# A state-space recurrence inside a decoder kernel: two 512-column units of its elementwise products in one instruction, and two subtractions moved from VectorE to GpSimd

## The chip, the cores and the metric

The kernel runs on one core of one Trainium2 chip (trn2). The metric is the device time of one execution in microseconds (us); a run of the kernel is timed three times and the median counts. The engines are TensorE (PE: matrix products, into the eight banks of PSUM), VectorE (DVE), ScalarE (ACT), GpSimd (POOL) and SyncE (SP), on whose queue every DMA of this kernel is issued, in program order. Every engine works off its own program in order; a semaphore wait holds all that stands behind it on that engine.

## The reference, cut to what matters

The input has 4 x 512 positions of 512 features. The layer in question is a Mamba mixer; behind it come its MLP, a quantized product layer and an FFN with 4-bit weights, which the change does not touch.

```python
zxbcdt = x @ in_proj_w.T                      # z, xv, Bm, Cm, dt_in
dt = softplus(dt_in @ dt_proj_w.T + dt_proj_b)
dA = exp(dt[..., None] * A)
dtx = dt * x_full
dBx = dtx[..., None] * Bg                     # the drive
def step(h, inp):
    h = dA_i * h + dBx_i                      # 1024 channels x 16 states
    y = einsum(C_i, h)                        # the read-out
y = ys + D_skip * x_full
```

## The kernel before

**Phases.** Layer norm and the first projections (to about 78 us), then the recurrence with the projections of the later batches beside it (78 to 1062 us), then output projection, MLP, quantized layer and FFN. The change lies in the recurrence and the DMA order beside it.

**Units and steps.** The recurrence is cut into 512 units of 128 partitions x 512 positions: 32 steps `g` (4 batches x 8 channel tiles) of 16 units `c` each, `n = 16 g + c`. For a unit, `spread_v` (TensorE) spreads dt*x over the partitions into PSUM bank 2 or 3, `spread_dt` spreads dt into bank 0 or 1, `decay` (ScalarE, L847) turns that into exp(A dt) in place, `make_drive` (VectorE, L1349) multiplies bank 2 or 3 by B into the ring `drive`, `scan` (VectorE, L1358) runs the recurrence into the ring `state` (6 units), `read_out` (GpSimd, L1172) multiplies by C into the ring `read` (8 units), and `gather_four` (TensorE, L1784) sums four units over the states. Once a step `skip_y` (L1369) makes `y`, and `soft_rest` (L1338, tile `sp_rest`) is the last instruction of VectorE in a step.

**The chain to the next step.** During step `g` the operands of step `g + 1` are made: GpSimd does `soft_sum`, `soft_dt` (dt), `dt_x` (dt*x), `dt_low` and `v_low` (the low halves of both), ScalarE between its exponentials `dt_high` (L837) and `v_high` (L841). SyncE then copies the halves into `dpack` and `vpack` (eight DMAs: `load_pack_dt`, `load_pack_v`), and the first `spread_v` of the next step waits for all eight. Ahead of them in SyncE's order stands `weights_after(first + 1)`, which in steps 0 to 3 stores a freshly split weight tile (`store_w`, L469) and waits for its low half.

**Low halves.** TensorE takes float32 operands as a rounded high half (ScalarE, `w_high`, `split_hi`) and the difference (VectorE before the change: `w_low` L1324, 13 instructions in steps 0 to 4; `split_lo` L1319, 4 in each of steps 3, 11 and 19).

All orders are written out by hand in the loops; nothing is scheduled by a planner.

## Time and profile before

| | |
|---|---|
| median of three runs | 2874.28 us (2871.49 to 2877.53) |
| the profiled execution | 2876.27 us, its span 2874.5 us |
| recurrence within the span | 78 to 1062 us |
| VectorE busy in the recurrence | 956.94 of 984.00 us |
| GpSimd busy in the recurrence | 870.46 us |
| TensorE busy in the recurrence | 839.67 us, mean granted clock 0.87 |

A busy time is the time with an instruction of that engine under way; idle time counts only where other work waits for the engine.

### The profile page before, as it was taken

Reading aid. Unit: us, or ns where it says so; the run is one execution under the profiler, and the core shown is the slowest. Engines: PE = TensorE matmul, PEld = TensorE weight load, DVE = VectorE, ACT = ScalarE, POOL = GpSimd, SP = SyncE. Lnnn points to the kernel's source line nnn. Section 1 sums busy time; section 2 is a strip of 40 time slices with the busy share of each in tenths; the row PEclk is TensorE's granted clock in tenths of the full one; section 3 lists DMA queues with packets and bytes.
Section 4 is the critical chain, followed back from the end, with each engine's and each line's share of the span. In section 5 each row is a group of like instructions: output and inputs, shape, how many; then the busy total and the mean of one; then the engine's idle time right before and its main releaser. Section 6 shows DMA issues by size and latency. Waiting matters only on the chain.

```text
span 2874.5 us, 32445 instructions
## 1 busy us (share of the span) xinstructions
PE 2651.7 (92%) x11096; PEld 1880.8 (65%) x11096; DVE 2129.6 (74%) x2731; ACT 1152.1 (40%) x1690; POOL 1255.9 (44%) x836
## 2 busy tenths in 40 slices
PE   7888888888899878999999999999989999999999
PEld 3443444444344326788887777887877788888887
DVE  4999999999999985543366677777767865555563
ACT  4555555555555534432244443443333322222221
POOL 2789888888889871110010023222212522222220
PEclk8998998989889769999999999999999999999999
DMA  6654654554465436221111112112111111111111
GB/s 230 209 157 121 188 157 121 157 166 129 132 183 154 133 99 231 81 76 49 52 66 59 45 37 67 44 45 67 44 37 45 44 49 48 51 45 52 50 47 66
DMA packets 152310, 275.35 MB, mean 96 GB/s; under 512 B 27345, under 2 KB 27857, under 8 KB 151633
## 3 DMA queue, kind: packets, MB, share of 16 engines
q1 hardware_dynamic: 152144, 273.27, 31.5%
q8 instruction: 88, 1.44, 0.2%
q14 instruction: 78, 0.63, 0.1%
HBM read 178.01 MB, written 61.34 MB: 83 GB/s over the span
## 4 chain that ended last, share of the span: by engine, by line
PE 71%; DVE 11%; ACT 9%; issue 5%; POOL 2%; DMA 1%; SPq 1%; DVEq 0%; POOLq 0%; ACTq 0%
PE ps L1733 19%; PE ps L1734 18%; PE ps L1735 18%; PE ps L1772 8%; DVE state L1358 6%; ACT ps L847 5%; PE ps L1784 4%; POOL read L1172 1%; DMA uraw<-y_d 1%; PE ps L1924 1%; PE ps L1868 1%; PE ps L1898 1%; DVE drive L1349 1%; DVE act_o L1677 0%; POOL xhr L1217 0%
## 5 line engine op out<-in xcount | busy, mean ns | idle before, releaser
L1172 POOL TENSOR_TENSOR read<-state,c_t 128x512 f32<-128x512 f32 x512 | 664.0, 1308 | 138.2 <-DVE state L1358 118.5
L1358 DVE TENSOR_TENSOR_SCAN state<-ps,drive 128x512 f32<-128x512 f32 x512 | 622.3, 1216 | 14.3 <-ACT ps L847 12.8
L1733 PE MATMUL ps<-xh,ghi 128*128 128x512 f32 x1536 | 609.1, 397 | 5.7 <-issue 5.7
L1231 POOL TENSOR_TENSOR wdeq<-packed,scales 128x1024 f32<-128x1024 f16 x96 | 260.2, 2711 | 798.3 <-DVE packed L1510 798.3
L1735 PE MATMUL ps<-xh,glo 128*128 128x512 f32 x1536 | 599.3, 390 | 0.0
L1734 PE MATMUL ps<-xl,ghi 128*128 128x512 f32 x1536 | 599.2, 390 | 0.0
L847 ACT ACTIVATE ps<-ps,a_exp 128x512 f32<-128x512 f32 x512 | 338.9, 662 | 473.8 <-PE ps L1772 472.5
L1772 PE MATMUL ps<-dpack,sel 128*128 128x512 f32 x512 | 260.9, 510 | 114.2 <-DVE state L1358 112.1
L1677 DVE TENSOR_TENSOR act_o<-act_o,ps 128x512 f32<-128x512 f32 x192 | 131.7, 686 | 313.4 <-PE ps L1735 298.5
L1349 DVE TENSOR_TENSOR drive<-ps,b_t 128x512 f32<-128x512 f32 x512 | 344.1, 672 | 12.7 <-PE ps L1772 11.9
L1099 ACT ACTIVATE ahi<-act_o 128x512 fp32r<-128x512 f32 x192 | 121.4, 632 | 562.6 <-DVE act_o L1677 562.6
L1733 PEld LDWEIGHTS ps<-xh,ghi 128*128 128x128 f32 x1536 | 289.4, 188 | 68.7 <-issue 9.2
L1734 PEld LDWEIGHTS ps<-xl,ghi 128*128 128x128 f32 x1536 | 289.4, 188 | 62.1 <-issue 3.1
L1735 PEld LDWEIGHTS ps<-xh,glo 128*128 128x128 f32 x1536 | 289.1, 188 | 60.7
L1733 PE MATMUL ps<-ahi,ghi 128*128 128x512 f32 x768 | 306.3, 399 | 20.2 <-issue 20.2
L1735 PE MATMUL ps<-ahi,glo 128*128 128x512 f32 x768 | 300.6, 391 | 0.0
L1734 PE MATMUL ps<-alo,ghi 128*128 128x512 f32 x768 | 300.6, 391 | 0.0
L1772 PE MATMUL ps<-vpack,sel 128*128 128x512 f32 x512 | 251.3, 491 | 28.6 <-DVE drive L1349 16.7
L1663 DVE TENSOR_TENSOR res<-res,ps 128x512 f32<-128x512 f32 x192 | 130.9, 685 | 192.6 <-PE ps L1735 190.0
L1772 PEld LDWEIGHTS ps<-dpack,sel 128*128 128x128 f32 x512 | 107.8, 211 | 244.1 <-DVE state L1358 235.3
L1772 PEld LDWEIGHTS ps<-vpack,sel 128*128 128x128 f32 x512 | 105.8, 207 | 225.2 <-DVE drive L1349 115.3
L965 ACT ACTIVATE ghi<-wdeq 128x1024 fp32r<-128x1024 f32 x96 | 100.9, 1051 | 297.7 <-POOL wdeq L1231 266.0
(204 smaller groups left out, 3775.3 us busy)
## 6 DMA issues: line engine op xcount, KB each, us to landing
whi<-w_d SPq DMA_DIRECT2D x63, 256.0 KB, 4.1
wlo<-w_d SPq DMA_DIRECT2D x63, 256.0 KB, 4.6
dpack<-dh SPq DMA_DIRECT2D x64, 128.0 KB, 3.8
dpack<-dl SPq DMA_DIRECT2D x64, 128.0 KB, 3.6
b_d<-ev SPq DMA_DIRECT2D x32, 256.0 KB
x_d<-ev SPq DMA_DIRECT2D x32, 256.0 KB, 2.6
vpack<-vh SPq DMA_DIRECT2D x64, 128.0 KB, 3.5
vpack<-vl SPq DMA_DIRECT2D x64, 128.0 KB, 2.8
```

Of the source, the lines that this page charges most:

```text
L847: act.activation(ps[:, n % 2, :], ps[:, n % 2, :], ACT.Exp, scale=a_exp[:, col:col + 1]).then_inc(decay_ready, 1)
L1099: act.activation(ahi[n // 2][:, cols(n % 2)], act_o[n % 2][:, :], ACT.Copy)\
L1172: pool.tensor_tensor(read[:, n % RRING, :], state[:, n % SRING, :], c_t[:, g % 2, :], ALU.mult).then_inc(read_ready, 1)
L1231: pool.tensor_tensor(wdeq[:, :].rearrange("p (h n) -> p h n", h=2), codes, scale, ALU.mult).then_inc(deq, 1)
L1349: dve.tensor_tensor(drive[:, n % DRING, :], ps[:, 2 + n % 2, :], b_t[:, g % 2, :], ALU.mult).then_inc(drive_ready, 1)
L1358: dve.tensor_tensor_scan(state[:, n % SRING, :], ps[:, n % 2, :], drive[:, n % DRING, :], 0.0, ALU.mult, ALU.add)\
L1663: dve.tensor_tensor(res[:, f, cols(b)], res[:, f, cols(b)], ps[:, free_bank(24 * E + 16 + k), :], ALU.add).then_inc(added, 1)
L1677: dve.tensor_tensor(act_o[n % 2][:, :], act_o[n % 2][:, :], ps[:, free_bank(24 * E + 2 * n + 1), :], ALU.mult)\
L1733: pe.matmul(out_, w_h, x_h, start=(start and k == 0), stop=False)
L1734: pe.matmul(out_, w_h, x_l, start=False, stop=False)
L1735: last = pe.matmul(out_, w_l, x_h, start=False, stop=(stop and k == n - 1))
L1772: pe.matmul(ps[:, bank, :], sel[:, 4 * (j % 2) + m, :], pack[j // 2][:, :], start=True, stop=True).then_inc(done, 1)
```

## The change

`make_drive` and `read_out` work on two units (a pair, `m` or `k`, 1024 columns) in one instruction; their semaphores count pairs (`PAIRS`, 8 a step). `spread_v` is issued for both units of the next pair at even `c`. `w_low` and `split_lo` inside the recurrence are GpSimd's now. On GpSimd `soft_dt` follows `soft_sum` behind pair 0, `dt_x` stands behind pair 1, `dt_low` behind pair 2, `v_low` behind pair 3. On ScalarE `dt_high` stands behind the exponential of unit 4 (it was 5), `v_high` behind that of unit 6 (it was 7). `drive` holds twice as much, for which `v_t`, `vh`, `vl` and the softplus tiles share places, with waits that follow from it. Two sums on the input tiles (`normalise`) move from steps 2 and 4 to 5 and 7.

```diff
 STEPS = B * CT
...
+    drive = place("drive", [P, DRING, 2, S], F32, after())
     state = place("state", [P, SRING, S], F32, after())
...
-    vh = place("vh", [P, S], F32R, after())
+    assert after() <= NORM_END, (after(), NORM_END)
+    vh = place("vh", [P, S], F32R, SP + 8192)
     vl = place("vl", [P, S], F32R, after())
-    assert after() <= NORM_END, (after(), NORM_END)
+    assert after() <= SP_END
 
 
...
@@ -801,12 +805,14 @@
                 act.wait_ge(dtp_ready, q + 1)
                 if q:
                     act.wait_ge(sp_exp_ready, q)
+                    act.wait_ge(sp_sum_ready, q)
...
-                    act.wait_ge(dt_ready, q)
+                    act.wait_ge(v_ready, q)
+                    act.wait_ge(dl_ready, q)
...
             def soft_log(q):
                 if q:
-                    act.wait_ge(dt_ready, q)
+                    act.wait_ge(vl_ready, q)
...
@@ -915,9 +921,9 @@
                     if jobs and c % 4 == 2 and c > 4:
                         take(first + c // 4 - 1)
                     if 0 <= g + 1 < STEPS:
-                        if c == 5:
+                        if c == 4:
                             dt_high(g + 1)
-                        if c == 7:
+                        if c == 6:
                             v_high(g + 1)
                     if nb < B:
                         if c == 12:
@@ -1130,17 +1136,12 @@
             def soft_dt(q):
                 pool.wait_ge(sp_sum_ready, q + 1)
                 pool.wait_ge(sp_pos_ready, q + 1)
-                if q:
-                    pool.wait_ge(dl_ready, q)
-                    pool.wait_ge(v_ready, q)
                 pool.tensor_tensor(dt_t[:, :], sp_log[:, :], sp_pos[:, :], ALU.add)\
                     .then_inc(dt_ready, 1)
 
             def dt_x(q):
                 pool.wait_ge(dt_ready, q + 1)
                 pool.wait_ge(x_t_loaded[q % 3], x_loads(q))
-                if q:
-                    pool.wait_ge(vl_ready, q)
                 pool.tensor_tensor(v_t[:, :], dt_t[:, :], x_t[:, q % 3, :], ALU.mult)\
                     .then_inc(v_ready, 1)
...
@@ -1160,17 +1161,31 @@
                 pool.tensor_tensor(owlo[:, part, :], owraw[:, part, :], owhi[:, part, :].bitcast(F32),
                                    ALU.subtract).then_inc(owlo_ready, 1)
 
-            def read_out(g, c):
-                n = NST * g + c
+            def read_out(g, k):
+
+                n = NST * g + 2 * k
                 if n == 0:
                     pool.wait_ge(res_stored, 16)
-                if c == 0:
+                if k == 0:
                     pool.wait_ge(c_loaded[g % 2], 16 * (g // 2 + 1))
-                pool.wait_ge(scan_done, n + 1)
+                pool.wait_ge(scan_done, n + 2)
                 if n >= RRING:
                     pool.wait_ge(gathered, (n - RRING) // 4 + 1)
-                pool.tensor_tensor(read[:, n % RRING, :], state[:, n % SRING, :], c_t[:, g % 2, :],
-                                   ALU.mult).then_inc(read_ready, 1)
+                at, src = n % RRING, n % SRING
+                pool.tensor_tensor(read[:, at:at + 2, :], state[:, src:src + 2, :],
+                                   over_tiles(c_t[:, g % 2, :], 2), ALU.mult).then_inc(read_ready, 1)
+
+            def split_lo(b, f):
+                pool.wait_ge(ln_hi, FT * b + f + 1)
+                pool.tensor_tensor(xl[b][:, f, :], xlr[b][:, f, :], xh[b][:, f, :].bitcast(F32),
+                                   ALU.subtract).then_inc(ln_lo, 1)
+
+            def w_low(n):
+                pool.wait_ge(whi_ready, n + 1)
+                pool.wait_ge(wlo_ready, n)
+                pool.tensor_tensor(wlo[n % 3][:, :, :], wraw[:, n % 2, :, :],
+                                   whi[n % 3][:, :, :].bitcast(F32), ALU.subtract)\
+                    .then_inc(wlo_ready, 1)
 
...
@@ -1182,22 +1197,27 @@
             for f in range(FT):
                 normalise(1, f)
             for g in range(STEPS):
-                for c in range(NST):
-                    read_out(g, c)
-                    if g in (2, 4) and c % 4 == 3:
-                        normalise(1 + g // 2, c // 4)
-                    if g in (STEPS - 3, STEPS - 2) and c in (12, 14):
-                        out_weights_low(2 * (g - STEPS + 3) + (c - 12) // 2)
+                nb, k_, jobs = step_jobs(g)
+                first = IN_TILES * nb + 3 * k_
+                for k in range(PAIRS):
+                    read_out(g, k)
+                    if g in (5, 7) and k % 2 == 1:
+                        normalise((g - 1) // 2, k // 2)
+                    if g in (CT - 5, 2 * CT - 5, 3 * CT - 5) and k % 2 == 1:
+                        split_lo(g // CT + 1, k // 2)
+                    if g in (STEPS - 3, STEPS - 2) and k in (6, 7):
+                        out_weights_low(2 * (g - STEPS + 3) + k - 6)
+                    if jobs and k % 2 == 1 and k < 6 and first + k // 2 + 2 < IN_TILES:
+                        w_low(first + k // 2 + 2)
                     if g + 1 < STEPS:
-                        if c == 0:
+                        if k == 0:
                             soft_sum(g + 1)
-                        if c == 1:
                             soft_dt(g + 1)
-                        if c == 2:
+                        if k == 1:
                             dt_x(g + 1)
-                        if c == 6:
+                        if k == 2:
                             dt_low(g + 1)
-                        if c == 8:
+                        if k == 3:
                             v_low(g + 1)
...
-            def make_drive(g, c):
-                n = NST * g + c
-                if c == 0:
+            def make_drive(m):
+
+                g = m // PAIRS
+                if m % PAIRS == 0:
                     dve.wait_ge(b_loaded[g % 2], 16 * (g // 2 + 1))
-                dve.wait_ge(vb_ready, n + 1)
-                if n >= DRING:
-                    dve.wait_ge(scan_done, n - DRING + 1)
-                dve.tensor_tensor(drive[:, n % DRING, :], ps[:, 2 + n % 2, :], b_t[:, g % 2, :],
+                dve.wait_ge(vb_ready, 2 * m + 2)
+                if m >= DRING:
+                    dve.wait_ge(scan_done, 2 * (m - DRING + 1))
+                dve.tensor_tensor(drive[:, m % DRING, :, :], ps[:, 2:4, :], over_tiles(b_t[:, g % 2, :], 2),
                                   ALU.mult).then_inc(drive_ready, 1)
...
-            def scan(g, c):
-                n = NST * g + c
-                dve.wait_ge(drive_ready, n + 1)
+            def scan(n):
+                dve.wait_ge(drive_ready, n // 2 + 1)
                 dve.wait_ge(decay_ready, n + 1)
                 if n >= SRING:
-                    dve.wait_ge(read_ready, n - SRING + 1)
+                    dve.wait_ge(read_ready, (n - SRING) // 2 + 1)
                 dve.tensor_tensor_scan(state[:, n % SRING, :], ps[:, n % 2, :],
-                                       drive[:, n % DRING, :], 0.0, ALU.mult, ALU.add)\
+                                       drive[:, n // 2 % DRING, n % 2, :], 0.0, ALU.mult, ALU.add)\
                    .then_inc(scan_done, 1)
...
-            make_drive(0, 0)
+            make_drive(0)
             for g in range(STEPS):
                 nb, k, jobs = step_jobs(g)
-                first = IN_TILES * nb + 3 * k
                 for c in range(NST):
-                    if c + 1 < NST:
-                        make_drive(g, c + 1)
-                    elif g + 1 < STEPS:
-                        make_drive(g + 1, 0)
-                    scan(g, c)
+                    n = NST * g + c
+                    if c % 2 == 0 and n // 2 + 1 < PAIRS * STEPS:
+                        make_drive(n // 2 + 1)
+                    scan(n)
                     for b in (1, 2, 3):
                         if g == CT * b - 6 and c % 4 == 1:
                             scale_x(b, c // 4)
-                        if g == CT * b - 5 and c % 4 == 2:
-                            split_lo(b, c // 4)
                     if g >= 1 and c == 6:
                         skip_y(g - 1)
-                    if jobs and c % 4 == 3 and c < 12 and first + c // 4 + 2 < IN_TILES:
-                        w_low(first + c // 4 + 2)
                     if nb and jobs and k == 0 and c == 6:
                         dt_split(nb)
...
                 if n >= 2:
-                    pe.wait_ge(drive_ready, n - 1)
+                    pe.wait_ge(drive_ready, n // 2)
...
             spread_v(0)
+            spread_v(1)
             for g in range(STEPS):
                 nb, k, jobs = step_jobs(g)
                 first = IN_TILES * nb + 3 * k
                 for c in range(NST):
                     n = NST * g + c
-                    if n + 1 < NST * STEPS:
-                        spread_v(n + 1)
+                    if c % 2 == 0 and n + 2 < NST * STEPS:
+                        spread_v(n + 2)
+                        spread_v(n + 3)
                     spread_dt(n)
                     if jobs and c < 12:
                         project(first + c // 4, c % 4)
```

GpSimd in step 1, before: from the last read-outs of step 0 on (`read` is `read_out`, `sp_log`, `dt_t`, `v_t`, `dl`, `vl` are the results of `soft_sum`, `soft_dt`, `dt_x`, `dt_low`, `v_low`).

```order
L1127 TENSOR_TENSOR sp_log<-sp_log,sp_rest 128x512
L1172 TENSOR_TENSOR read<-state,c_t 128x512
L1136 TENSOR_TENSOR dt_t<-sp_log,sp_pos 128x512
L1172 TENSOR_TENSOR read<-state,c_t 128x512
L1144 TENSOR_TENSOR v_t<-dt_t,x_t 128x512
L1172 TENSOR_TENSOR read<-state,c_t 128x512 x4
L1149 TENSOR_TENSOR dl<-dt_t,dh 128x512
L1172 TENSOR_TENSOR read<-state,c_t 128x512 x2
L1154 TENSOR_TENSOR vl<-v_t,vh 128x512
```

GpSimd at the same place of the changed kernel.

```order
L1175 TENSOR_TENSOR read<-state,c_t 128x1024 x3
L1133 TENSOR_TENSOR sp_log<-sp_log,sp_rest 128x512
L1139 TENSOR_TENSOR dt_t<-sp_log,sp_pos 128x512
L1175 TENSOR_TENSOR read<-state,c_t 128x1024
L1186 TENSOR_TENSOR wlo_83<-wraw,whi_80 128x512
L1145 TENSOR_TENSOR v_t<-dt_t,x_t 128x512
L1175 TENSOR_TENSOR read<-state,c_t 128x1024
L1150 TENSOR_TENSOR dl<-dt_t,dh 128x512
L1175 TENSOR_TENSOR read<-state,c_t 128x1024
L1186 TENSOR_TENSOR wlo_81<-wraw,whi_78 128x512
L1155 TENSOR_TENSOR vl<-v_t,vh 128x512
```

One instruction now reads out two units, `dt_t` has moved ahead of the second read-out, and three weight subtractions (`wlo`) stand between, one ahead of `v_t` and one ahead of `vl`.

ScalarE in step 1, before: `ps<-ps,a_exp` are the exponentials, `dh` and `vh` the copies for `dt_high` and `v_high`.

```order
L847 ACTIVATE ps<-ps,a_exp 128x512 x3
L781 ACTIVATE whi_80<-wraw 128x512
L847 ACTIVATE ps<-ps,a_exp 128x512 x3
L837 ACTIVATE dh<-dt_t 128x512
L847 ACTIVATE ps<-ps,a_exp 128x512
L781 ACTIVATE whi_78<-wraw 128x512
L798 ACTIVATE ev<-ps 128x512
L847 ACTIVATE ps<-ps,a_exp 128x512
L841 ACTIVATE vh<-v_t 128x512
```

ScalarE at the same place of the changed kernel.

```order
L853 ACTIVATE ps<-ps,a_exp 128x512 x3
L785 ACTIVATE whi_80<-wraw 128x512
L853 ACTIVATE ps<-ps,a_exp 128x512 x2
L843 ACTIVATE dh<-dt_t 128x512
L853 ACTIVATE ps<-ps,a_exp 128x512 x2
L785 ACTIVATE whi_78<-wraw 128x512
L802 ACTIVATE ev<-ps 128x512
L847 ACTIVATE vh<-v_t 128x512
L853 ACTIVATE ps<-ps,a_exp 128x512 x4
```

`dh` now stands behind the fifth exponential of the step and not the sixth, `vh` behind the seventh and not the eighth.

SyncE in step 1 of the changed kernel, from the store of a weight tile to the pack copies; with other line numbers the order of before reads the same.

```order
L473 DMA w_d<-whi_78 128x512 [waits wlo_ready]
L474 DMA w_d<-wlo_81 128x512
L456 DMA wraw<-in_in_w 128x512
L524 DMA dpack_99<-dh 64x512 [waits dh_ready,dtb_ready]
L525 DMA dpack_100<-dh 64x512
L527 DMA dpack_99<-dl 64x512 [waits dl_ready]
L528 DMA dpack_100<-dl 64x512
L524 DMA vpack_103<-vh 64x512 [waits vh_ready,vb_ready]
L525 DMA vpack_104<-vh 64x512
L527 DMA vpack_103<-vl 64x512 [waits vl_ready]
L528 DMA vpack_104<-vl 64x512
```

The order has not moved, but `wlo_ready`, for which the first row waits, is now signalled by GpSimd.

## Rows read from the trace of the kernel before

**Rows 1.** The page: its head and part 1 (engines, busy time, share of the span).

```profile
span 2874.5 us, 32445 instructions
...
PE 2651.7 (92%) x11096; PEld 1880.8 (65%) x11096; DVE 2129.6 (74%) x2731; ACT 1152.1 (40%) x1690; POOL 1255.9 (44%) x836
```

**Rows 2.** Windows: recurrence (78 to 1062 us) and what follows; columns as in the second line.

```profile
core 0: us, PE busy (x) PEld busy (x) DVE busy (x) ACT busy (x) POOL busy (x), PEclk, DMA share, GB/s
78.00:1062.00 984.00, 839.67 (x3060) 419.94 (x3058) 956.94 (x1124) 511.44 (x831) 870.46 (x678) 0.87 0.52 150
1062.00:2874.50 1812.50, 1756.53 (x7888) 1430.28 (x7888) 1133.89 (x1554) 601.15 (x794) 366.14 (x142) 0.98 0.19 61
```

**Rows 3.** Groups of VectorE, 78 to 1062 us: busy us, mean ns | idle before.

```profile
L1358 DVE TENSOR_TENSOR_SCAN state<-ps,drive 128x512 f32<-128x512 f32 x512 | 622.3, 1216 | 14.3 <-ACT ps L847 12.8 <-POOL read L1172 1.1 <-DVE drive L1349 0.3
L1349 DVE TENSOR_TENSOR drive<-ps,b_t 128x512 f32<-128x512 f32 x511 | 343.5, 672 | 12.7 <-PE ps L1772 11.9
...
L1324 DVE TENSOR_TENSOR wlo<-wraw,whi 128x512 fp32r<-128x512 f32 x13 | 12.6, 969 | 0.0
L1319 DVE TENSOR_TENSOR xl<-xlr,xh 128x512 fp32r<-128x512 f32 x12 | 11.9, 994 | 0.0
```

**Rows 4.** Waits, 78 to 1062 us: who for whom, us in total, times, longest.

```profile
DVE state L1358 <- ACT ps L847: 12.8, 30, 0.8
DVE drive L1349 <- PE ps L1772: 11.9, 20, 0.7
...
DVE state L1358 <- POOL read L1172: 1.1, 2, 0.9
```

**Rows 5.** Timeline of VectorE, one undisturbed pair of units: start us, duration us.

```profile
633.00 0.67 DVE L1349 TENSOR_TENSOR drive<-ps,b_t 128x512 f32<-128x512 f32 x1
633.59 1.22 DVE L1358 TENSOR_TENSOR_SCAN state<-ps,drive 128x512 f32<-128x512 f32 x1
634.72 0.67 DVE L1349 TENSOR_TENSOR drive<-ps,b_t 128x512 f32<-128x512 f32 x1
```

**Rows 6.** Groups of GpSimd, 78 to 1062 us.

```profile
L1172 POOL TENSOR_TENSOR read<-state,c_t 128x512 f32<-128x512 f32 x511 | 662.8, 1308 | 138.2 <-DVE state L1358 118.5 <-PE ps L1784 15.9
...
L1160 POOL TENSOR_TENSOR owlo<-owraw,owhi 128x1024 fp32r<-128x1024 f32 x4 | 9.5, 2366 | 0.0
```

**Rows 7.** Groups after 1062 us: a VectorE product of 1024 columns.

```profile
L1439 DVE TENSOR_TENSOR uraw<-uraw,zraw 128x1024 f32<-128x1024 f32 x16 | 19.7, 1239 | 34.9 <-ACT zraw L938 34.9
```

**Rows 8.** Timeline of ScalarE, the copy of dt between two exponentials.

```profile
618.84 0.62 ACT L837 ACTIVATE dh<-dt_t 128x512 fp32r<-128x512 f32 x1
619.40 0.66 ACT L847 ACTIVATE ps<-ps,a_exp 128x512 f32<-128x512 f32 x1
```

**Rows 9.** Timeline of TensorE and VectorE at the start of a step.

```profile
608.50 1.94 PE L1784 MATMUL ps<-read,gather 128*32 128x512 f32 x8
...
610.95 0.63 PE L1772 MATMUL ps<-dpack,sel 128*128 128x512 f32 x1
...
612.37 1.22 DVE L1358 TENSOR_TENSOR_SCAN state<-ps,drive 128x512 f32<-128x512 f32 x1 [0.48 <-ACT ps L847]
```

**Rows 10.** Timeline of the DMA queue on SyncE in step 2.

```profile
159.39 0.32 SPq L469 DMA_DIRECT2D w_d<-whi  x1
...
160.78 0.47 SPq L520 DMA_DIRECT2D dpack<-dh  x1
...
165.21 0.60 SPq L524 DMA_DIRECT2D vpack<-vl  x1
```

**Rows 11.** GpSimd and TensorE timelines in steps 2 and 16, and landings of vpack.

```profile
162.94 1.74 POOL L1154 TENSOR_TENSOR vl<-v_t,vh 128x512 fp32r<-128x512 f32 x1
...
604.38 0.50 PE L1772 MATMUL ps<-vpack,sel 128*128 128x512 f32 x1 [0.82 <-DMA vpack<-vl]
...
DMA to landing us min/median/max: 2.2/3.0/5.8
```

**Rows 12.** Timeline of VectorE: `sp_rest`, the end of steps 0, 3, 15 and 16.

```profile
107.61 0.66 DVE L1338 SCALAR_TENSOR_TENSOR sp_rest<-ps,sp_exp 128x512 f32<-128x512 f32 x1
...
211.34 0.66 DVE L1338 SCALAR_TENSOR_TENSOR sp_rest<-ps,sp_exp 128x512 f32<-128x512 f32 x1
...
577.97 0.68 DVE L1338 SCALAR_TENSOR_TENSOR sp_rest<-ps,sp_exp 128x512 f32<-128x512 f32 x1
...
608.05 0.68 DVE L1338 SCALAR_TENSOR_TENSOR sp_rest<-ps,sp_exp 128x512 f32<-128x512 f32 x1
```

More of the change, by code:

```diff
@@ L41 @@
 DRING, SRING, RRING = 3, 6, 8
+PAIRS = NST // 2
 STEPS = B * CT
@@ L109, in build @@
     gather = place("gather", [P, NST // 4, P // 4], F32, after())
-    sp_abs = place("sp_abs", [P, S], F32, after())
-    sp_pos = place("sp_pos", [P, S], F32, after())
-    sp_exp = place("sp_exp", [P, S], F32, after())
-    sp_log = place("sp_log", [P, S], F32, after())
-    sp_rest = place("sp_rest", [P, S], F32, after())
-    dt_t = place("dt_t", [P, S], F32, after())
-    row_r = place("row_r", [P, S], F32, after())
+    SP = after()
+    sp_abs = place("sp_abs", [P, S], F32, SP)
+    sp_rest = place("sp_rest", [P, S], F32, SP)
+    sp_pos = place("sp_pos", [P, S], F32, SP + 2048)
+    dt_t = place("dt_t", [P, S], F32, SP + 2048)
+    sp_log = place("sp_log", [P, S], F32, SP + 4096)
+    v_t = place("v_t", [P, S], F32, SP + 4096)
+    sp_exp = place("sp_exp", [P, S], F32, SP + 6144)
+    SP_END = SP + 12288
+    row_r = place("row_r", [P, S], F32, SP_END)
     row_u = place("row_u", [P, S], F32, after())
@@ L126, in build @@
     y_t = place("y_t", [P, 2, S], F32, FREE0)
-    drive = place("drive", [P, DRING, S], F32, after())
+    drive = place("drive", [P, DRING, 2, S], F32, after())
     state = place("state", [P, SRING, S], F32, after())
@@ L626, in _ @@
                     store_hat(1)
-                if g in (4, 6):
-                    store_hat(g // 2)
+                if g in (7, 9):
+                    store_hat((g - 3) // 2)
                 if 0 <= g + 1 < STEPS:
@@ L1777, in gather_four @@
                 n = NST * g + 4 * m
-                pe.wait_ge(read_ready, n + 4)
+                pe.wait_ge(read_ready, n // 2 + 2)
                 if m == 0 and g:
```

5 lines of the change are left out of this document (2 added, 3 removed).

## The prediction

> **What bounds the kernel now.** I read the windows first: in the recurrence VectorE is busy 956.94 of 984.00 us, GpSimd 870.46, TensorE 839.67, and what follows (1812.5 us) is not touched [rows 1, 2]. Then the groups of VectorE: 512 scans of 1216 ns and 511 drives of 672 ns are nearly all of it, and the idle time ahead of them is 14.3 and 12.7 us [rows 3]. So a VectorE nanosecond saved here is a nanosecond of the kernel, if nobody else becomes late. Busy times overlap at their ends, so the price of an instruction is its distance to the next start: drive at 633.00, scan at 633.59, next drive at 634.72, that is 0.58 to 0.59 for a drive, 1.13 for a scan, 3.42 for two units [rows 5]. The waits say who is late today: ScalarE 12.8 us, TensorE 11.9 us, GpSimd 1.1 us [rows 4]. At the start of step 17 it lies behind the gather at the step's start, which took 1.94 us: the spreads behind it are late, and the scan of unit 1 comes 0.48 us late for its exponential [rows 9]. A plain step takes 608.05 - 577.97 = 30.08 us [rows 12].
>
> **What it takes away.** Pairing: a product of 1024 columns took 1239 ns [rows 7] where two of 512 take 1344. But starts count: a drive of 672 is followed after 0.58, so 0.09 of its end is covered; 1239 less 0.09 is 1.15 against 2 x 0.58 = 1.16. That row reads two SBUF tiles, the drive one of PSUM, so it may be a little quicker. I take 1.12, 0.04 saved: 256 x 0.04 = 10 us. Bounds: 0.01 x 256 = 3 us, and the whole fixed part by the two durations, 0.105 x 256 = 27 us. The subtractions: 13 of 969 ns and 12 of 994 ns [rows 3], less 0.09 overlap each, 13 x 0.88 + 12 x 0.90 = 22 us off VectorE. Together -32.
>
> A rule speaks for the upper end. The Trainium skill, page "VectorE: DVE Perf Modes", section "The TRN2 errata — SBUF-src ops pay a fixed extra latency per instruction", gives a float32 product (N + 151) cycles at 0.96 GHz and says that one large tile pays the fixed part once. By it 256 merged drives would save 40 us and the sum would be -2. The durations here come near it (672 for 512 columns), but the starts [rows 5] show most of the fixed part beside its neighbour, and the trace decides.
>
> **What it adds on ScalarE: dt arrives after it is asked for.** Count from the start of the scan of unit 1, S1 = 0, at VectorE's own pace: drive pair at 1.13, S2 2.25, S3 3.38, drive pair 4.5, S4 5.6, S5 6.75. GpSimd may read out pair 0 when S1 has ended, 1.22 + 0.08 = 1.30. A paired read-out costs between 2.37 (the 128x1024 subtraction) and 2 x 1.31 [rows 6]; I take 2.42. `soft_sum` and `soft_dt`, of the size of an unpaired read-out (mean 1.31 with its disturbed ones), follow at 1.28 each: dt is there at 6.3. ScalarE meets `dt_high` behind the exponential of unit 4 (S2 ends at 3.5, spread and exponential take 0.5 to 0.63 and 0.66 [rows 8, 9]: done near 4.8), and in-order it waits, copies for 0.56 [rows 8], and does unit 5's exponential from 6.9 to 7.55; S5 starts at 7.65, not 6.75. That is 0.9 us of idle VectorE. Before, dt needed only unit 0, then unit 1, and was asked for one unit later: copy and exponential follow each other without idle [rows 8]. It happens in 31 steps; in two of them (10, 18) a `scale_x` behind unit 1 covers it: 29 x 0.9 = 26 us. It costs nothing if GpSimd were 0.9 us quicker, and 1.1 x 31 = 34 us if the read-out takes 2.62.
>
> **`v_high`, one link on.** In plain steps dt*x is there at 10.0, `v_high` ends 10.6, unit 7's exponential 11.25, and S7 is due at 11.7 (`skip_y` gives 0.64): hidden. Where GpSimd has one more 1.25 us operation behind pair 1 (steps 0 to 5, 7, 11, 19: `w_low`, `normalise`, `split_lo`) S7 is 0.9 late: 9 x 0.9 = 8 us. Step 3 has both and is 1.25 later again (counted below).
>
> **The pack copies in steps 0 to 3.** VectorE's `w_low` stood behind unit 7; now it is behind pair 3 on a GpSimd that is itself late: pair 0 1.3, sum and dt to 6.3, pair 1 8.7, `wlo` 9.95, dt*x 11.2, pair 2 13.6, `dl` 14.9, pair 3 17.3, `wlo` 18.6. SyncE waits for that `wlo` ahead of the eight pack copies. In step 2 the store is issued at 159.39 and the last `vl` copy at 165.21 [rows 10]: 5.8 us, so 24.4; landing 2.2 to 5.8, median 3.0 [rows 11]: about 27.5. The first `spread_v` of the next step now stands at c = 14, ahead of VectorE's drive there: due 22.2 + 0.9 + 0.9 = 24.0 less what `skip_y` had already given, 23.1. Late by 4.4; four steps 17 us, of which `scale_x` in step 2 covers 3, and step 3, 2.5 later on GpSimd, adds 3: +17. In other steps `v_low` is done at 17.3 (19.8 where loaded), its copies land at 21 to 23: today TensorE waits for them now and then without cost to VectorE (one at 604.38, 0.82 us) [rows 11], then some 1 us in all.
>
> **Smaller.** At a step's start unit 1's exponential is due 0.58 earlier than before (no drive between S0 and S1), and the `spread_v` between gather and `spread_dt` (the gather ends at 610.44, the `spread_dt` starts at 610.95) is gone [rows 9]: net 0 to 0.25, taken 0.15 x 31 = 5 us. Begin and end: the first scan now waits for two pairs of spreads and drives (+2), the last pair's read-out is 1.1 longer (+1): +3. GpSimd's load itself: 8 x 2.42 + 5 x 1.27 = 25.7 a step, 29.5 with three `wlo`, 34.5 in step 3; `state` holds six units, enough for about 5 us behind, so only step 3 (counted) presses. `dt` and `sp` tiles that share places add waits whose partners are done units before.
>
> **The sum.** -10 - 22 + 26 + 8 + 17 + 1 + 5 + 3 = +28 us. Against the profiled execution's 2876.3 that is 2904; the median of the runs shown is 2 us lower, so 2902.
>
> **The rivals.**
> - *Faster.* GpSimd delivers dt before 5.4 (pair read-out about 1.5 us) and the pack copies are in time: -32 + 8 = -24, 2850. For it: VectorE really loses 32 us of work, and its idle today is small. Against it: no 128x1024 row of GpSimd is under 2.3 us. The deciding point is S1 + 5.4. 0.14.
> - *One of the two stalls holds.* Only ScalarE's: +11, 2885. Only the pack copies': +2, 2876. For it: TensorE's own lateness at unit 5 may cover part of the 0.9, and step 0 to 3 have slack that I can have counted wrongly by 2 us. 0.18.
> - *The fixed part of each merged drive is saved whole.* That is -27 for -10: with all stalls +11, 2885. Against it: the starts [rows 5]. By the rule of the Trainium skill above, with its 40 us, it would be 2872. 0.06.
> - *GpSimd becomes the bound.* If its operations stretch beside VectorE (the same kind took 1.74 us at 162.94 [rows 11]), paired read-outs near 2.7 make 28 to 32 a step and dt later by 0.3: 2915 to 2930. 0.07.
> - *The forecast,* both stalls, 2888 to 2915: 0.55.
>
> **How the numbers follow.** A measurement here tells about 0.2% (6 us) from no change. Faster: 0.14, a third of the partial cases (0.05) and little else, 0.20. Same: the rest of the cases near 2876, 0.12. Slower: 0.68. The range takes in the partial cases and the slower half of the faster one at the lower end, and half of GpSimd's at the upper: 2862 to 2920; the forecast's own is 2888 to 2915.
>
> **What would show it.** Right: plain steps 30.5 to 31 us between `sp_rest` starts (30.08 now), 0.7 to 1 us of VectorE idle for ScalarE ahead of the scan of unit 5 in each, ScalarE's `dh` waiting for GpSimd's `dt_t`; steps 0 to 3 near 36 us (on average 34.6 between the first and fourth end now [rows 12]), with the drive at c = 14 waiting for TensorE, and that for `vpack<-vl`. Drives of 1.20 to 1.24 us, paired read-outs of 2.4 to 2.6. Wrong: `dh` without idle ahead of it, or starts two scans and a drive apart of well under 3.38; then VectorE's saving comes through.

## The result and the profile after

The changed kernel takes 2909.8 us (median of four runs, 2908.8 to 2911.04); the kernel before took 2874.35 us beside it (2871.49 to 2877.53). The ratio is 1.0123, with a 95% interval of 1.0106 to 1.0141: 35 us slower. The forecast was 2902, range 2862 to 2920.

First the page's head of the changed kernel, then its windows, cut where the last `y_t` starts (1094.8 us; 1065.6 before), and those of the kernel before with the same cut.

```profile
span 2907.4 us, 31438 instructions
```

```profile
core 0: us, PE busy (x) PEld busy (x) DVE busy (x) ACT busy (x) POOL busy (x), PEclk, DMA share, GB/s
78.00:1094.80 1016.80, 820.04 (x3072) 405.39 (x3070) 922.24 (x843) 506.23 (x832) 851.24 (x448) 0.88 0.50 145
1094.80:2907.40 1812.60, 1757.80 (x7880) 1432.79 (x7880) 1135.98 (x1553) 601.21 (x793) 364.76 (x140) 0.98 0.20 61
```

```profile
78.00:1065.60 987.60, 841.61 (x3068) 420.14 (x3066) 957.07 (x1125) 511.69 (x831) 872.00 (x679) 0.87 0.52 149
1065.60:2874.50 1808.90, 1754.60 (x7880) 1430.07 (x7880) 1133.76 (x1553) 600.90 (x793) 364.61 (x140) 0.99 0.19 61
```

VectorE did lose work: 957.07 to 922.24, 34.8 us. But its time without work in the recurrence went from 30.5 (987.60 - 957.07) to 94.6 us (1016.80 - 922.24). So the recurrence is 29.2 us longer, and 3.7 us came behind it. Where VectorE stands idle, its groups say (76 to 1100 us: busy us, mean ns | idle before), beside [rows 3]:

```profile
L1378 DVE TENSOR_TENSOR_SCAN state<-ps,drive 128x512 f32<-128x512 f32 x512 | 608.3, 1212 | 60.0 <-issue 55.8 <-ACT ps L853 4.1
L1370 DVE TENSOR_TENSOR drive<-ps,b_t 128x1024 f32<-128x1024 f32 x256 | 308.3, 1204 | 30.5 <-issue 29.7 <-PE ps L1786 0.8
```

Ahead of the scans 14.3 us have become 60.0, ahead of the drives 12.7 have become 30.5. The view puts both down to "issue", which names nobody; who was late has to be read from the other engines' waits:

```profile
PE ps L1786 <- DMA vpack<-vl: 56.5, 21, 6.7
DVE state L1378 <- issue: 55.8, 73, 2.6
ACT dh L843 <- POOL dt_t L1139: 51.2, 31, 3.1
ACT vh L847 <- POOL v_t L1145: 47.6, 31, 2.8
```

ScalarE now waits for dt in all 31 steps (51.2 us) and for dt*x in all 31 (47.6), TensorE for the pack copies 21 times, up to 6.7 us (7 times, 6.6 us in all, before).

**One plain step, the scan of unit 5.** Timelines of GpSimd, ScalarE and VectorE in step 16 (start us, duration us).

```profile
600.57 2.38 POOL L1175 TENSOR_TENSOR read<-state,c_t 128x1024 f32<-128x1024 f32 x1 [2.05 <-DVE state L1378]
602.91 1.29 POOL L1133 TENSOR_TENSOR sp_log<-sp_log,sp_rest 128x512 f32<-128x512 f32 x1
604.28 1.29 POOL L1139 TENSOR_TENSOR dt_t<-sp_log,sp_pos 128x512 f32<-128x512 f32 x1
```

```profile
603.27 0.66 ACT L853 ACTIVATE ps<-ps,a_exp 128x512 f32<-128x512 f32 x1 [1.58 <-PE ps L1786]
605.59 0.63 ACT L843 ACTIVATE dh<-dt_t 128x512 fp32r<-128x512 f32 x1 [1.66 <-POOL dt_t L1139]
606.13 1.30 ACT L853 ACTIVATE ps<-ps,a_exp 128x512 f32<-128x512 f32 x2
```

```profile
600.36 1.20 DVE L1370 TENSOR_TENSOR drive<-ps,b_t 128x1024 f32<-128x1024 f32 x1
601.47 2.33 DVE L1378 TENSOR_TENSOR_SCAN state<-ps,drive 128x512 f32<-128x512 f32 x2
603.72 1.20 DVE L1370 TENSOR_TENSOR drive<-ps,b_t 128x1024 f32<-128x1024 f32 x1
604.83 1.21 DVE L1378 TENSOR_TENSOR_SCAN state<-ps,drive 128x512 f32<-128x512 f32 x1
606.86 1.22 DVE L1378 TENSOR_TENSOR_SCAN state<-ps,drive 128x512 f32<-128x512 f32 x1 [0.82 <-issue]
```

Read out, sum, dt: dt_t ends at 605.57, and at 605.59 the waiting copy `dh` starts. Behind it in ScalarE's order stands the exponential of unit 5, at 606.13. Its scan comes at 606.86, 0.82 us late. Where nobody is late, a pair goes 600.36, 601.47, 603.72: 3.36 us. Before it was 3.42, by the mean distances of undisturbed starts (0.58 from a drive to the scan, 1.13 from a scan to the drive).

Even so a plain step is no longer than before. Steps 13 to 17 take 149.59 us in the changed kernel (the starts of `sp_rest` below) and 149.58 before (488.56 to 638.14), single steps 29.3 to 30.7: there the 0.82 us at unit 5 is given back by the pairing and by a shorter wait at the step's start.

```profile
506.53 0.67 DVE L1358 SCALAR_TENSOR_TENSOR sp_rest<-ps,sp_exp 128x512 f32<-128x512 f32 x1
...
656.12 0.67 DVE L1358 SCALAR_TENSOR_TENSOR sp_rest<-ps,sp_exp 128x512 f32<-128x512 f32 x1
```

**The end of step 0: the copies are issued late.** GpSimd, the DMA queue on SyncE, TensorE, then VectorE.

```profile
98.37 1.29 POOL L1186 TENSOR_TENSOR wlo<-wraw,whi 128x512 fp32r<-128x512 f32 x1
99.62 1.28 POOL L1155 TENSOR_TENSOR vl<-v_t,vh 128x512 fp32r<-128x512 f32 x1
```

```profile
99.69 0.32 SPq L473 DMA_DIRECT2D w_d<-whi  x1
...
101.02 0.48 SPq L524 DMA_DIRECT2D dpack<-dh  x1
...
105.42 0.60 SPq L528 DMA_DIRECT2D vpack<-vl  x1
```

```profile
108.28 1.22 PE L1786 MATMUL ps<-vpack,sel 128*128 128x512 f32 x2 [5.68 <-DMA vpack<-vl]
```

```profile
109.59 1.23 DVE L1370 TENSOR_TENSOR drive<-ps,b_t 128x1024 f32<-128x1024 f32 x1 [4.50 <-issue]
```

The subtraction ends at 99.66, and at 99.69 the weight store that waited for it opens the queue for the copies. The last copy is issued at 105.42, though `vl` was ready at 100.90; TensorE spreads at 108.28 and VectorE's drive is 4.50 us late. At the ends of steps 1 to 3, which have the same store, it is 4.25, 1.55 and 5.55 us late: 15.9 us with step 0.

**The end of step 20: the copies land late.** From step 4 on there is no such store. In its place, in most steps, `weights_after` loads two halves of a weight tile, 256 KB each, ahead of the copies. The drive is 4.03 us late at the end of step 4 and 9.8 us in all at seven later ends; step 20 is the longest of these.

```profile
736.97 0.45 SPq L488 DMA_DIRECT2D wlo<-w_d  x1
...
742.01 0.60 SPq L528 DMA_DIRECT2D vpack<-vl  x1
748.35 1.22 PE L1786 MATMUL ps<-vpack,sel 128*128 128x512 f32 x2 [3.52 <-DMA vpack<-vl]
749.66 1.23 DVE L1370 TENSOR_TENSOR drive<-ps,b_t 128x1024 f32<-128x1024 f32 x1 [2.34 <-issue]
```

```profile
742.00:748.00 6.00, 2.70 (x14) 0.84 (x12) 5.32 (x5) 2.88 (x5) 4.79 (x3) 0.95 1.01 255
```

GpSimd ended `vl` at 741.48 and the last copy was issued at once, 0.53 us later. But it landed only at 748.30, 6.3 us on, while the DMA engines were busy all the time (share 1.01 from 742 to 748 us). Where the loads stand behind the copies (run 3), the same copy landed after 2.7 us.

Of the 64 us of new idle time ahead of drives and scans, by place: 24.7 us stand ahead of unit 5's scan, 7.5 ahead of unit 7's, 29.7 ahead of the drive that waits for the copies, 5.4 at other units; the step's start has 3.8 less.

### The profile page after: what moved, and what is told of

It reads as the page before. It is cut to its first block, busy times and chain, and to the rows that moved or that the text cites. A ratio compares the mean times of both kernels' runs of the same rounds, so it can differ in the third digit from the quotient of the medians.

```text
span 2907.4 us, 31438 instructions
## 1 busy us (share of the span) xinstructions
PE 2631.4 (91%) x11096; PEld 1868.3 (64%) x11096; DVE 2097.0 (72%) x2450; ACT 1146.4 (39%) x1690; POOL 1235.3 (42%) x605
## 4 chain that ended last, share of the span: by engine, by line
PE 63%; issue 11%; DVE 9%; POOL 8%; ACT 4%; DMA 3%; SPq 1%; POOLq 0%; DVEq 0%; ACTq 0%
PE ps L1747 18%; PE ps L1749 18%; PE ps L1748 18%; DVE state L1378 4%; PE ps L1786 4%; POOL read L1175 3%; PE ps L1798 3%; DMA vpack<-vl 2%; POOL sp_log L1133 1%; ACT ps L853 1%; POOL v_t L1145 1%; DMA uraw<-y_d 1%; DVE drive L1370 1%; PE ps L1940 1%; PE ps L1914 1%
## 5 line engine op out<-in xcount | busy, mean ns | idle before, releaser
L1175 POOL TENSOR_TENSOR read<-state,c_t 128x1024 f32<-128x1024 f32 x256 | 611.8, 2392 | 184.4 <-DVE state L1378 182.2
L1378 DVE TENSOR_TENSOR_SCAN state<-ps,drive 128x512 f32<-128x512 f32 x512 | 608.3, 1212 | 60.0 <-issue 55.8
L1370 DVE TENSOR_TENSOR drive<-ps,b_t 128x1024 f32<-128x1024 f32 x256 | 308.3, 1204 | 30.5 <-issue 29.7
L1748 PEld LDWEIGHTS ps<-xl,ghi 128*128 128x128 f32 x1536 | 289.6, 189 | 62.1 <-issue 3.1
L1786 PE MATMUL ps<-vpack,sel 128*128 128x512 f32 x512 | 197.0, 470 | 102.6 <-DMA vpack<-vl 56.5
L1698 DVE TENSOR_TENSOR alo<-act_o,ahi 128x512 fp32r<-128x512 f32 x192 | 152.8, 796 | 67.7 <-ACT ahi L1105 66.3
```

Of the source, the lines that this page charges most:

```text
L1175: pool.tensor_tensor(read[:, at:at + 2, :], state[:, src:src + 2, :], over_tiles(c_t[:, g % 2, :], 2), ALU.mult).then_inc(read_ready, 1)
L1370: dve.tensor_tensor(drive[:, m % DRING, :, :], ps[:, 2:4, :], over_tiles(b_t[:, g % 2, :], 2), ALU.mult).then_inc(drive_ready, 1)
L1378: dve.tensor_tensor_scan(state[:, n % SRING, :], ps[:, n % 2, :], drive[:, n // 2 % DRING, n % 2, :], 0.0, ALU.mult, ALU.add)\
L1698: dve.tensor_tensor(alo[n // 2][:, cols(n % 2)], act_o[n % 2][:, :], ahi[n // 2][:, cols(n % 2)].bitcast(F32), ALU.subtract)\
L1748: pe.matmul(out_, w_h, x_l, start=False, stop=False)
L1786: pe.matmul(ps[:, bank, :], sel[:, 4 * (j % 2) + m, :], pack[j // 2][:, :], start=True, stop=True).then_inc(done, 1)
```

## The experiments

Ratios are against the kernel before, timed on the same chip beside each run. "Idle" is VectorE's ahead of drives and of scans in its groups from 76 to 1100 us; the changed kernel has 30.5 and 60.0, the kernel before 12.7 and 14.3. They are those of one execution, the profiled one.

| kernel | median us | ratio, 95% interval | idle: drives, scans |
|---|---|---|---|
| changed kernel | 2909.80 | 1.0123 (1.0106 to 1.0141) | 30.5, 60.0 |
| 1 ScalarE's copies one unit later | 2899.71 | 1.0081 (1.0056 to 1.0105) | 48.2, 40.0 |
| 2 `w_low` back on VectorE | 2893.81 | 1.0067 (1.0051 to 1.0083) | 12.8, 52.1 |
| 3 pack copies ahead of the weights | 2875.83 | 1.0003 (0.9994 to 1.0013) | 2.6, 59.5 |
| 4 dt ahead of the first read-out | 2889.04 | 1.0052 (1.0036 to 1.0067) | 31.1, 42.4 |
| 5 pairing alone | 2887.67 | 1.0044 (1.0028 to 1.0059) | 13.5, 36.8 |
| 6 low halves alone | 2866.21 | 0.9969 (0.9956 to 0.9982) | 18.9, 16.8 |
| 7 kernel before with 3's order | 2875.45 | 1.0002 (0.9993 to 1.0011) | 13.5, 14.4 |
| 8 edits 3 and 4 together | 2854.84 | 0.9928 (0.9911 to 0.9944) | 2.3, 39.1 |
| 9 only the drives paired | 2884.30 | 1.0044 (1.0027 to 1.0061) | 12.2, 33.6 |
| 10 edit 3 on kernel 6 | 2867.31 | 0.9977 (0.9967 to 0.9987) | 19.5, 16.2 |
| 11 kernel 8, dt*x one pair earlier | 2856.66 | 0.9948 (0.9933 to 0.9963) | 6.4, 38.9 |
| 12 edit 3 on kernel 5 | 2873.57 | 1.0003 (0.9994 to 1.0013) | 3.0, 35.8 |

**1. ScalarE's copies back to where they were.**

```diff
-                        if c == 4:
+                        if c == 5:
                             dt_high(g + 1)
-                        if c == 6:
+                        if c == 7:
                             v_high(g + 1)
```

> The changed kernel with one edit: ScalarE's dt_high back behind the exponential of unit 5 and v_high behind that of unit 7. Theory (three late arrivals: dt on ScalarE, dt*x on ScalarE, pack copies on TensorE): the 0.82 us of VectorE idle ahead of unit 5 goes in 31 steps (25 us) and the 0.7 us ahead of unit 7 in nine steps (6 us), while the pack copies, due against a faster VectorE, cost some 0.8 to 1.5 us more in about ten steps: 2909.8 - 31 + 10 = 2889, 2882 to 2897. Rival (GpSimd's load of paired read-outs sets the pace, and ScalarE's wait only shows it): the idle moves to other places, 2904 to 2911.

Measured 2899.7, above the range I gave; two of its four executions took 2904 us, two 2893 to 2895, and the idle times are those of one at 2904. The scans of units 5 and 7 lost 27.5 us of idle time, nearly the expected 31, but the scans of unit 1 gained 6, and the drives 17.7. The drive at the ends of steps 1 to 4 waits 5.78, 3.25, 7.69 and 5.40 us, against 4.25, 1.55, 5.55 and 4.03. In these steps the last copy lands no earlier than in the changed kernel (254.50 us at the end of step 4, 252.74 there), and VectorE was only there earlier: where the copies end the wait, what is saved ahead of them is lost.

**2. The weights' low halves back on VectorE in steps 0 to 4.**

```diff
-                    if jobs and k % 2 == 1 and k < 6 and first + k // 2 + 2 < IN_TILES:
-                        w_low(first + k // 2 + 2)      # GpSimd
...
+                    if jobs and c % 4 == 3 and c < 12 and IN_TILES * nb + 3 * k + c // 4 + 2 < IN_TILES:
+                        w_low(IN_TILES * nb + 3 * k + c // 4 + 2)      # VectorE
```

> The changed kernel with one edit: the 13 weight subtractions w_low of steps 0 to 4 back on VectorE behind units 3, 7 and 11; split_lo stays on GpSimd. Theory: the wait for the pack copies made in steps 0 to 4 (4.5, 4.3, 1.6, 5.6, 4.0 us of VectorE idle, 20 us) shrinks to what the other steps have (about 1 us each), unit 7's 0.7 us goes in these steps, and VectorE does 13 x 0.65 to 0.88 us more: 2909.8 - 15 - 3 + 10 = 2902, 2895 to 2906; the gain in steps 0 to 4 is there to see in the step lengths. Rival (the pack wait is the earlier deadline at unit 14 alone, not w_low): the idle stays and the kernel is 10 us slower, 2918 to 2922.

Measured 2893.8, just below the range: the drives' idle time fell by 17.7 us and the scans' by 7.9, for about 11 us of work put back. At the ends of steps 0 to 3 the drive has no wait left, for 15.9 us; at the end of step 4 1.75 us are left, and at the later ends 9.6 us of 9.8. So `w_low` on GpSimd is the cause in steps 0 to 3, and the later waits have another.

**3. The pack copies ahead of the weights in SyncE's order,** with `w_low` still on GpSimd.

```diff
-                if jobs:
-                    weights_after(first + 1)
                 if 0 <= g + 1 < STEPS:
                     load_pack_dt(g + 1)
                     load_pack_v(g + 1)
                 if jobs:
+                    weights_after(first + 1)
                     spill(first + 1)
```

> The changed kernel with one edit on SyncE: the eight pack copies are issued ahead of weights_after(first + 1), the store of a weight tile, instead of behind it. Theory (the store's wait for the w_low on GpSimd holds the copies): in steps 0 to 3 the last vl copy is issued about 3.4 us sooner, as soon as v_low ends, and 3 us of idle goes in each: 2909.8 - 12 = 2898, 2893 to 2902. Rival (GpSimd's own lateness with v_low is the cause, and SyncE's order hides nothing): 2906 to 2911.

Measured 2875.8, 34 us below the changed kernel: the largest single step, and far outside what either theory gave it. The queue on SyncE of this kernel at the same place, and VectorE:

```profile
94.92 0.85 SPq L524 DMA_DIRECT2D dpack<-dh  x1
...
100.78 0.60 SPq L528 DMA_DIRECT2D vpack<-vl  x1
101.42 0.59 SPq L473 DMA_DIRECT2D w_d<-whi  x1
```

```profile
104.35 1.20 DVE L1369 TENSOR_TENSOR drive<-ps,b_t 128x1024 f32<-128x1024 f32 x1
```

The last copy is issued 4.6 us earlier (100.78 for 105.42) and the drive of 109.59 starts at 104.35 without a wait. `sp_rest` of step 4 starts at 236.75 instead of 257.94, 21 us by then. Another 10 come in the later steps. There `weights_after` puts two loads ahead of the copies, and in this run behind them; from issue to landing the copies of `vpack` take, in the changed kernel and in this one:

```profile
DMA to landing us min/median/max: 2.2/3.2/7.2
```

```profile
DMA to landing us min/median/max: 2.2/2.4/3.9
```

The remaining 3 us lie behind the recurrence. The scans' idle time did not move (59.5): the two causes are separate in place.

**4. `soft_sum` and `soft_dt` ahead of the first paired read-out.**

```diff
                 for k in range(PAIRS):
+                    if k == 0 and g + 1 < STEPS:
+                        soft_sum(g + 1)
+                        soft_dt(g + 1)
                     read_out(g, k)
...
-                        if k == 0:
-                            soft_sum(g + 1)
-                            soft_dt(g + 1)
```

> The changed kernel with one edit on GpSimd: soft_sum and soft_dt stand ahead of the read-out of pair 0, where GpSimd is idle, instead of behind it; its work is the same. Theory: dt is there 2.5 us sooner than ScalarE asks for it (25 us of idle ahead of unit 5 go), dt*x and v_low come 1.5 us sooner (unit 7's 6 us go, the pack waits fall by a little under 1 us each): 2909.8 - 25 - 6 - 8 = 2871, 2862 to 2882. Rival (GpSimd's load sets the pace): the work is the same, 2904 to 2911.

Measured 2889.0, 21 us below the changed kernel and short of the expected range. Ahead of the scans of unit 5 20.5 us went, and in a plain step of kernel 8, which has the same edit, `dh` has no wait left:

```profile
600.35 0.62 ACT L842 ACTIVATE dh<-dt_t 128x512 fp32r<-128x512 f32 x1
```

But only 3.4 of the expected 6 us went at unit 7, none of the 8 at the copies (29.6 for 29.7), and the scans of unit 1 wait 6.8 us more.

**5 and 6. Each half alone.** Kernel 5 is kernel 1 with `w_low` and `split_lo` back on VectorE; kernel 6 is the kernel before with only these on GpSimd:

```diff
                 for c in range(NST):
                     read_out(g, c)
+                    if g in (CT - 5, 2 * CT - 5, 3 * CT - 5) and c % 4 == 3:
+                        split_lo(g // CT + 1, c // 4)
+                    if jobs and c % 4 == 3 and c < 12 and first + c // 4 + 2 < IN_TILES:
+                        w_low(first + c // 4 + 2)
```

> The pairing alone: the changed kernel with w_low and split_lo back on VectorE and dt_high and v_high back behind units 5 and 7. The paired drive takes 1.11 between starts where two took 1.16 to 1.17, 15 us less in all. Theory (the pairing itself brings the lateness of dt and of the pack copies, since all copies are now due at unit 14): the copies' wait costs 1 to 3 us in about ten steps, 15 to 20 us, as much as is saved: 2876 - 15 + 18 = 2879, 2871 to 2888. Rival (the low halves on GpSimd are the whole of the loss, the pairing is a gain): 2857 to 2864.

> The other part alone: the kernel before, unpaired, with w_low and split_lo of the recurrence on GpSimd behind the read-outs of units 3, 7, 11 (and 15). VectorE has 22 us less. Theory: in steps 0 to 3 the store on SyncE waits for the w_low behind unit 7 and the pack copies come 1 to 3 us late against a deadline at unit 15, 8 us in all; the rest is gained: 2876 - 22 + 8 = 2862, 2854 to 2871. Rival (putting them on GpSimd is what makes the changed kernel slow): 2880 and more.

Both in their ranges, kernel 5 at the upper edge of its own (2888). Pairing alone is 12 us slower, low halves alone 9 us faster; their sum is +3. Together, in kernel 1, they are +24, and the whole change, which also has ScalarE's copies one unit earlier, is +35. The low halves are a gain where the read-outs are single and a loss where they are paired: between kernels 5 and 1 the same move costs 12 us. With single read-outs the drive at the step's end is late for the copies by 7.3 us in all (kernel 6), with paired ones by 46.8 (kernel 1) and 29.7 (the changed kernel).

**7. Edit 3 on the kernel before.**

> The kernel before with the SyncE edit of e3_sp_order alone, a control. Theory: before the change TensorE's waits for the pack copies hardly reach VectorE (11.9 us of drive idle lies at unit 2, behind the gather), so the order changes nothing: 2872 to 2878. Rival (the order is a gain of its own, not the mending of what the change brought): 2850 to 2862.

2875.45 against 2875.48: no gain. So edit 3 takes back a loss that the change brings, and is not a gain of its own.

**8. Edits 3 and 4 together.**

> The changed kernel with the edits of e3_sp_order and e6_dt_first together: pack copies ahead of the store on SyncE, soft_sum and soft_dt ahead of pair 0 on GpSimd. Theory: the two remove different waits (drive at unit 14; scan of unit 5 and in nine steps of unit 7), so the gains of 34 and 21 us add: 2875.8 - 21 to 25 = 2852, 2845 to 2860, faster than both kernels. Rival (they take away the same wait, which only shows in two places): 2868 to 2876.

2854.8, 0.7% under the kernel before (55 us under the changed kernel; apart, the edits took 34 and 21). The paired kernel pays if both waits are taken away; it is then also 11 us faster than kernel 6, which has the low halves alone.

**9. Only the drives paired,** read-outs single, GpSimd in the order of before:

```diff
-            def read_out(g, k):
-                n = NST * g + 2 * k
+            def read_out(g, c):
+                n = NST * g + c
...
-                pool.wait_ge(scan_done, n + 2)
+                pool.wait_ge(scan_done, n + 1)
```

> Only the drives are paired: read-outs one unit at a time, GpSimd's order, ScalarE's order and the low halves on VectorE as in the kernel before; spread_v is issued two units ahead, so all pack copies are due at unit 14. Theory (the deadline at unit 14 is what costs; v_low stands behind unit 8's read-out, 1.3 us later than in the pair order): 1 to 1.5 us of drive idle in most steps, 30 us, less 15 saved on VectorE: 2890, 2882 to 2898. Rival (the paired read-outs on GpSimd are the costly half): 2858 to 2868.

2884.3, in the range, at the same ratio as kernel 5 (1.0044 both): the paired read-out is not the costly half of pairing. But the theory behind the range had 30 us of drive idle; there are 12.2, and 33.6 ahead of the scans, so the number came out and the reason only in part. (The execution with these idle times, at 2879.5, was the fastest of four.)

**10. Edit 3 on kernel 6.**

> e5_low_only (unpaired, low halves on GpSimd) with the pack copies ahead of the store on SyncE. Theory: the 7.3 us of drive idle at unit 15 for the copies of steps 0 to 3 go, nothing else changes: 2866.2 - 8 = 2858, 2853 to 2863. Rival (the rest of the gain that the low halves did not give, 22 less 9, lies in GpSimd's load): 2864 to 2868.

2867.3, no better than kernel 6 and above the range. The idle time of the drives that wait for the copies fell from 7.3 to 2.3 us, that of the drives at unit 2 rose from 7.8 to 12.8, which is about what the kernel before has there (12.3). This wait goes with TensorE's granted clock at a step's start, of which the last section speaks: it was low (mean under 0.6) at 16 step starts of kernel 6, at 20 of kernel 10 and at 18 of the kernel before.

**11. Kernel 8 with `dt_x` behind pair 0 instead of pair 1.**

```diff
                     if g + 1 < STEPS:
-                        if k == 1:
+                        if k == 0:
                             dt_x(g + 1)
```

> e9_sp_and_dt with one edit: dt_x behind pair 0 instead of pair 1 on GpSimd. Theory: ScalarE's remaining 13.9 us of waits for dt*x go; VectorE has some 5 us of idle for them ahead of units 6 and 7: 2854.8 - 4 = 2851, 2847 to 2855. Rival (they hide behind something else): 2854 to 2857.

2856.7, no gain. The 4.5 us ahead of the scans of unit 7 did go (0.1 left), but unit 1 waits 2.3 us more and the drives at the step's end 4.1 us more, so that the sum stayed. The wait for dt*x is a small part of what is left and is worth nothing by itself.

**12. Edit 3 on kernel 5,** pairing alone with its copies in time.

> e4_pair_only (pairing of drives and read-outs, everything else as before) with the pack copies ahead of the store on SyncE. Theory: the 12 us of drive idle at unit 14 go, the pairing then gives what is left of its 15 us after the later dt*x on ScalarE: 2887.7 - 13 = 2875, 2868 to 2880. Rival (the pairing costs something that no wait shows): 2882 and more.

2873.6, in the range. The drives' idle is 3.0, the scans' 35.8, against 12.7 and 14.3 before: pairing shortens 256 pairs by about 0.06 us (15 us) and gives 12 us net back in waits; it is worth nothing by itself, as its ratio says (1.0003, 0.9994 to 1.0013).

## Why the prediction was right, and where its terms were off

Direction came as forecast, and so did two of the mechanisms: dt late on ScalarE ahead of unit 5's scan, and the pack copies of steps 0 to 3 late behind GpSimd's `w_low`. Runs 3 and 4 take them away one by one, run 8 both. The third, the late landing of the copies in later steps, was not foreseen. One of the signs that the prediction named did not come: plain steps were to take 30.5 to 31 us and take 29.9 on the mean, as before. The loss lies in the steps whose copies are late.

Idle time of VectorE by place, in us. "Start" is the scan of unit 1 and the drive of the unit or pair after it, "copies" the drive that waits for the pack copies:

| kernel | start | unit 5 | unit 7 | copies | rest | sum |
|---|---|---|---|---|---|---|
| before | 22.6 | 3.1 | 0.0 | 0.0 | 1.3 | 27.0 |
| changed | 18.8 | 27.8 | 7.5 | 29.7 | 6.7 | 90.5 |
| 3 | 22.7 | 27.3 | 7.6 | 1.1 | 3.4 | 62.1 |
| 4 | 26.1 | 7.3 | 4.1 | 29.6 | 6.4 | 73.5 |
| 8 | 26.1 | 7.3 | 4.5 | 0.9 | 2.6 | 41.4 |
| 12 | 26.0 | 7.1 | 0.0 | 1.6 | 4.1 | 38.8 |

The terms of the sum:

- **Pairing, -10 us.** Drives last 1204 ns and their scans start 1.12 us on, as I took, for 2 x 0.58 before; the scans are followed by the next drive 0.015 us sooner too. A pair is 3.36 for 3.42: 0.06 x 256 = -15. The rival with the fixed part saved whole is out. The Trainium skill, page "VectorE: DVE Perf Modes", section "The TRN2 errata — SBUF-src ops pay a fixed extra latency per instruction", would have it at 40 us, an estimate from its fixed 151 cycles. This trace agrees with it nearly in the durations, where the busy time of drives fell by 35 us (511 x 672 to 256 x 1204 ns [rows 3]), and not in the time: starts gained 15, since most of the fixed part had been beside a neighbour already.
- **Low halves off VectorE, -22.** With the drives' overlap, VectorE's busy time fell by 34.8 against 32 predicted. Alone they gave 9 us (run 6), not 22: that kernel has 8.7 us more idle time (18.9 and 16.8 for 12.7 and 14.3). The 13 us that this leaves are there in the recurrence, which is 12 us shorter; 3 us are lost again behind it.
- **dt late, +26.** Unit 5's 0.82 us in nearly every step is the 0.9 of the forecast, 24.7 us in all. In steps 2, 10 and 18, which `scale_x` was to cover, 0.5 us are left.
- **dt*x late in steps with one more operation, +8.** Eight steps (0, 1, 3, 4, 5, 7, 11, 19) show 0.58 to 1.98 us at unit 7: 7.5.
- **Pack copies in steps 0 to 3, +17.** 15.9 us. The 5.8 us from the store to the last copy came out (5.73 to 5.78 in these steps), but with some luck: in the rows it was read from, the last copy waited for `vl`, ready at 164.68 [rows 10, 11], and not for the queue.
- **Pack copies in the other steps, +1.** This was the mis-sized step: 13.8 us (4.03 and 9.8). I had the copies land 3.0 us after their issue, the median, in every step. In the eight steps in question, all with the two loads ahead of them, the last one takes 5.1 to 7.2 us, and VectorE, whose drive needs it at unit 14 already, waits. The order of run 3, in which the landing falls to a median of 2.4 us, takes these waits away together with the others.
- **Step starts, +5.** 18.8 us for 22.6 before: -3.8. In the kernels where the waits ahead of it are gone it is 22.7 to 26.1, so up to +3.5.
- **Other units,** for which I had no term: +5.4, 3.8 of it ahead of the scan behind the late drive (unit 15).
- **Begin and end, +3:** the first scan is 1.6 us later and the last `y_t` waits 4.47 for 3.47, so +2.6.
- **Behind the recurrence, 0:** it is 3.7 longer (1812.60 for 1808.90), with 0.01 less of TensorE's granted clock and 3.2 us more TensorE busy time. No run was aimed at it; the code is the same in all kernels of this case, and from the last `y_t` on they take 1807.9 to 1812.6 us, so it is not shown to come from the change.

The sum of the terms as measured by place (-15 -22 +24.7 +7.5 +15.9 +13.8 -3.8 +5.4 +2.6 +3.7) is +32.8; the spans differ by 32.9. That the forecast's +28 lies near it owes something to errors that cancel: the later copies and the other units cost 18 us more than I had, the step starts and the pairing 14 us less. Removing the stalls (34 and 21 us) gives 4 to 6 us more than their idle times; about 3 of each lie behind the recurrence. In the rivals, the pack copies alone should have stood at some -6 and not at +2, since the 8 us of dt*x fall away with ScalarE's lateness too.

**What stays open.** Run 8 has 41.4 us of idle time for 27.0 before. Most of it, 26.1 us, stands at the step's start, where the kernel before has 22.6; the last section shows what it goes with. New are 4.2 us at unit 5 and 4.5 at unit 7, and run 11 turns the latter into other waits. What still holds unit 5, 0.1 us in most steps and 0.9 in five, was not tried.

## What to carry to other kernels

Moving work off the busiest engine pays only as far as its new place is not ahead of something with a due time: here one subtraction on GpSimd in each of four steps delayed a store on SyncE's in-order queue, and eight copies behind the store reached TensorE up to 6.7 us late. Ask of each operation made longer or moved what is queued behind its consumer, and put the transfers with the nearest due time ahead in the queue. That holds for their data too: copies issued in time landed 5 to 7 us later behind 512 KB of loads that had more time. Here two changes of order turned 1.2% slower into 0.7% faster. Price a merged instruction by the distance between starts, not by the durations.
